# Feed-forward stages: token mean and 1/deviation as high/low product pairs, sums earlier in VectorE's order

## What is computed

```python
def _layernorm(x, axis=-1, eps=1e-05):
    m = jnp.mean(x, axis=axis, keepdims=True)
    v = jnp.var(x, axis=axis, keepdims=True)
    return (x - m) / jnp.sqrt(v + eps)

x_prev = jnp.concatenate([jnp.zeros((B, 1, C), x.dtype), x[:, :-1, :]], axis=1)
xr = mu_r * x + (1.0 - mu_r) * x_prev
xk = mu_k * x + (1.0 - mu_k) * x_prev
r = jax.nn.sigmoid(jnp.einsum('btc,dc->btd', xr, W_r))
k = jnp.einsum('btc,dc->btd', xk, W_k)
k_act = jnp.square(jax.nn.relu(k))
out = r * jnp.einsum('btc,dc->btd', k_act, W_v)

x = x + 0.5 * ffn(_layernorm(x))        # ffn_phase "ffn1"
x = x + attention(_layernorm(x))
x = x + 0.5 * ffn(_layernorm(x))        # ffn_phase "ffn2"
```

## Time and profile before

| | |
|---|---|
| median of 3 runs | 3531.27 us (3527.9 to 3531.66) |
| profiled execution | 3538.78 us |
| its span, first to last instruction | 3536.9 us |
| mean granted clock of TensorE | 0.972 of full |
| busy over the span: PE, DVE, ACT, POOL | 93%, 78%, 45%, 52% |
| matmuls, DVE, ACT, POOL instructions | 83236, 4491, 2344, 1707 |

### The profile page before, as it was taken

The page is one execution under the profiler, slowest core; times in us unless marked ns, Lnnn a source line. Parts: engine busy times, 40 slices in busy tenths (PEclk is TensorE's granted clock), DMA queues, the critical chain, the costliest instruction groups (busy, mean ns, idle before and its releaser), DMA issues. The chain is left out here.

```text
span 3536.9 us, 191423 instructions
## 1 busy us (share of the span) xinstructions
PE 3288.2 (93%) x83236; PEld 2760.8 (78%) x83236; DVE 2753.6 (78%) x4491; ACT 1583.4 (45%) x2344; POOL 1823.7 (52%) x1707
## 2 busy tenths in 40 slices
PE   7999998799999999995999999999996987999999
PEld 5888886576767767674999999999995765888887
DVE  6767775787888878784899999999997856676765
ACT  4455553577777777772112211221113433545454
POOL 1232322566555665654777888888874431223232
PEclk8999999899999999997999999999998998999999
DMA  3122212232323323225777777777774772212121
GB/s 119 71 97 81 101 77 95 74 99 82 103 73 92 93 74 99 86 76 133 187 198 199 200 199 199 203 201 197 200 197 149 228 221 99 107 71 107 71 107 59
DMA packets 486525, 452.84 MB, mean 128 GB/s; under 512 B 55488, under 2 KB 448832, under 8 KB 467264
## 3 DMA queue, kind: packets, MB, share of 16 engines
q1 hardware_dynamic: 484160, 449.56, 42.0%
q10 hardware_dynamic: 2304, 2.49, 0.3%
HBM read 331.33 MB, written 120.60 MB: 128 GB/s over the span
## 5 line engine op out<-in xcount | busy, mean ns | idle before, releaser
L350 POOL TENSOR_TENSOR ffn_out<-ffn_gate,ffn_xres 128x512 f32<-128x512 f32 x128 | 182.1, 1451 | 784.2 <-DVE ffn_gate L254 783.8
L784 DVE SCALAR_TENSOR_TENSOR ain_conv<-ain_padded,ain_taps,ain_conv 128x512 f32<-128x512 f32 x384 | 416.5, 1085 | 13.8 <-DVE ain_tail L781 0.3
L1464 ACT ACTIVATE rec_u<-rec_ps_end 128x256 f32<-128x256 f32 x128 | 49.2, 384 | 631.0 <-PE rec_ps_end L1516 631.0
L885 POOL TENSOR_TENSOR ain_conv<-ain_conv,ain_term 128x512 f32<-128x512 f32 x192 | 272.3, 1418 | 16.0
L1232 POOL TENSOR_TENSOR rec_d_norm<-rec_dmat,rec_early 128x512 f32<-128x512 f32 x128 | 162.7, 1271 | 174.8 <-DVE rec_dmat L1314 174.8
L940 ACT ACTIVATE ain_buf<-ain_conv 128x512 f32<-128x512 f32 x192 | 121.0, 630 | 232.3 <-POOL ain_conv L885 146.7
L46 PE MATMUL ffn_ring<-ffn_mixkh,ffn_wkh 128*128 128x512 f32 x512 | 218.4, 427 | 6.5 <-DVE ffn_mixkl L196 6.5
L46 PE MATMUL ffn_ring<-ffn_mixrh,ffn_wrh 128*128 128x512 f32 x512 | 215.4, 421 | 9.2 <-DVE ffn_mixrl L306 9.2
L46 PE MATMUL ffn_ring<-ffn_mixkh,ffn_wkl 128*128 128x512 f32 x512 | 203.2, 397 | 0.0
L46 PE MATMUL ffn_ring<-ffn_mixrh,ffn_wrl 128*128 128x512 f32 x512 | 202.0, 395 | 0.0
L46 PE MATMUL ffn_ring<-ffn_act_h,ffn_wvh 128*128 128x512 f32 x512 | 201.8, 394 | 0.0
(11 more groups left out here) (249 smaller groups left out, 10285.6 us busy)
## 6 DMA issues: line engine op xcount, KB each, us to landing
rec_early<-coeffs SPq DMA_DIRECT2D x512, 128.0 KB, 3.0
streams<-ain_buf SPq DMA_DIRECT2D x48, 1024.0 KB, 5.1
rec_qkv<-streams SPq DMA_DIRECT2D x126, 384.0 KB, 3.3
rec_qk_pe<-streams SPq DMA_DIRECT2D x127, 256.0 KB, 3.4
rec_late<-coeffs SPq DMA_DIRECT2D x504, 64.0 KB, 2.3
ffn_xres<-in_x SPq DMA_DIRECT2D x16, 1024.0 KB
ain_x<-x SPq DMA_DIRECT2D x16, 1024.0 KB, 4.9
gate<-ain_gate SPq DMA_DIRECT2D x16, 1024.0 KB, 6.7
```

The lines of the kernel that those rows point to most:

```text
L350: added = nc.gpsimd.tensor_tensor(out[:, m, :], gate[:, m, :], xres[:, m, :], ALU.add)
L784: nc.vector.scalar_tensor_tensor(out=out[:], in0=pad[:, n:n + TOK], scalar=taps[:, u // KT, u % KT, n:n + 1], in1=out[:], op0=ALU.mult, op ...
L885: nc.gpsimd.tensor_tensor(out[:], out[:], term[:], ALU.add).then_inc(pool_conv, 1)
L1464: nc.scalar.activation(u[:], ps_end[:, :, 1, :], ACT.Copy).then_inc(u_ready, 1)
```

## The change

The mean (from tile 2 on) and the spread of 1/deviation (all tiles) become two `float32r` matmuls each. Their moving operand is split into a high and a low part, and the constant operand is a `float32r` copy. ACT rounds `sum1` into `sum_h`, between its roundings of mix r and mix k; DVE subtracts. The four reciprocals per partition are split by two small DVE instructions, and the diagonal tile is twice as wide. DVE's `sums` goes ahead of `act_rest` 3, and the new `sum_rest` stands where `sums` stood.

```diff
+            dve.wait_ge(consts, 1)
+            nc.vector.tensor_copy(mean_r[:], mean_w[:])
+            nc.vector.tensor_copy(ones_r[:], ones[:])
...
+            def sum_rest(t):
+                dve.wait_ge(sum_high, t - 1)
+                nc.vector.tensor_tensor(sum_l[:], sum1[:], sum_h[:].bitcast(F32), ALU.subtract).then_inc(sum_split, 1)
...
                 dve.wait_ge(inverted, t + 1)
-                nc.vector.tensor_tensor(rstd_diag[:], ident[:].unsqueeze(1).to_broadcast([P, KT, P]),
-                                        rstd_tok[:].unsqueeze(2).to_broadcast([P, KT, P]), ALU.mult).then_inc(diagonal, 1)
+                nc.vector.tensor_copy(rstd_split[:, 0, :], rstd_tok[:]).then_inc(rstd_high, 1)
+                dve.wait_ge(rstd_high, t + 1)
+                nc.vector.tensor_tensor(rstd_split[:, 1, :], rstd_tok[:], rstd_split[:, 0, :].bitcast(F32),
+                                        ALU.subtract).then_inc(rstd_low, 1)
+                dve.wait_ge(rstd_low, t + 1)
+                nc.vector.tensor_tensor(rstd_diag[:], ident[:].unsqueeze(1).unsqueeze(1).to_broadcast([P, 2, KT, P]),
+                                        rstd_split[:].bitcast(F32).unsqueeze(3).to_broadcast([P, 2, KT, P]),
+                                        ALU.mult).then_inc(diagonal, 1)
...
                 act_rest(t, 2)
+                if ahead == 2:
+                    sums(t + 2)
                 act_rest(t, 3)
                 if ahead:
                     mix_rest(t + 1, "r", 0)
                 if ahead == 2:
-                    sums(t + 2)
+                    sum_rest(t + 2)
...
+            def sum_round(t):
+                act.wait_ge(summed, t)
+                act.wait_ge(mean_done, t)
+                nc.scalar.activation(sum_h[:], sum1[:], ACT.Copy).then_inc(sum_high, 1)
...
             def mean(t):
-                pe.wait_ge(summed, t)
-                nc.tensor.matmul(ps_mean[:], mean_w[:], sum1[:], start=True, stop=True).then_inc(mean_done, 1)
+                if isinstance(t, int) and t == 1:
+                    pe.wait_ge(summed, 1)
+                    nc.tensor.matmul(ps_mean[:], mean_w[:], sum1[:], start=True, stop=True).then_inc(mean_done, 1)
+                else:
+                    pe.wait_ge(sum_split, t - 1)
+                    nc.tensor.matmul(ps_mean[:], mean_r[:], sum_h[:], start=True, stop=False)
+                    nc.tensor.matmul(ps_mean[:], mean_r[:], sum_l[:], start=False, stop=True).then_inc(mean_done, 1)
...
-                nc.tensor.matmul(ps_rstd[:], ones[:], rstd_diag[:].rearrange("p j n -> p (j n)"), start=True,
-                                 stop=True).then_inc(spread, 1)
+                for part in range(2):
+                    last = nc.tensor.matmul(ps_rstd[:], ones_r[:], rstd_diag[:, part].rearrange("p j n -> p (j n)"),
+                                            start=(part == 0), stop=(part == 1))
+                last.then_inc(spread, 1)
```

More of the change, by code:

```diff
@@ L90, in ffn_phase @@
         var_tok, std_tok, rstd_tok = (sb(n, [P, KT]) for n in ("var_tok", "std_tok", "rstd_tok"))
-        rstd_diag = sb("rstd_diag", [P, KT, P])
+        rstd_diag = sb("rstd_diag", [P, 2, KT, P], F32R)
+        rstd_split = sb("rstd_split", [P, 2, KT], F32R)
+        sum_h, sum_l = sb("sum_h", [P, TOK], F32R), sb("sum_l", [P, TOK], F32R)
+        mean_r, ones_r = sb("mean_r", [P, P], F32R), sb("ones_r", [P, P], F32R)
         ps_mean = ctx.enter_context(nc.psum_tensor(f"{tag}_mean", [P, TOK], F32))
@@ L108, in ffn_phase @@
         v_used, out_ready = sem("v_used"), sem("out_ready")
+        sum_high, sum_split, rstd_high, rstd_low = sem("sum_high"), sem("sum_split"), sem("rstd_high"), sem("rstd_low")
         x0_loaded, r_loaded = [sem(f"x0_loaded{k}") for k in range(2)], sem("r_loaded")
@@ L407, in slot @@
                     high(t + 1, "r", 0)
+                if more == 2:
+                    sum_round(t + 2)
                 if more:
@@ L438, in _ @@
             high(0, "k", 1)
-            with act.Fori(0, NT - 1) as t:
-                slot(t, True)
-            slot(NT - 1, False)
+            with act.Fori(0, NT - 2) as t:
+                slot(t, 2)
+            slot(NT - 2, 1)
+            slot(NT - 1, 0)
         @block.tensor
```

## The result

The changed kernel takes 3540.59 us in the median of 20 runs, the kernel before 3529.07 us in 20 runs beside them. The ratio is 1.0023, 95% interval [1.0016, 1.0029]: slower by 5.6 to 10.2 us, with 8.1 in the middle. The forecast was +8.4 us and 3539.7.

What follows compares the result with a forecast made beforehand. PE was taken to bound a feed-forward slot; 23.5 us spared, 30.0 of new waits and 1.9 at the starts gave +8.4 us on the 3531.3 median, 3539.7 us. The range was 3533 to 3546.

Steps and rivals of the forecast that it cites:

- Matmuls: Mean and spread on PE: two float32r matmuls cost 0.46 us instead of 0.86, sparing 23.5 us in all.
- The reciprocal's chain: DVE between var and spread: two more steps and a wider diagonal, 0.95 us more, hidden in the loop.
- The start of each phase: At each feed-forward phase's start the 0.95 us of longer DVE chain is paid in full: 1.9 us.
- The sums, moved: Sums ahead of DVE's fourth low part make PE wait 1.07 us in effect in 28 slots: 30.0 us.
- Sum: Both feed-forward phases together: -23.5 + 30.0 + 1.9 = +8.4 us, or 3539.7 us against the median.
- the first rival: PE stays the bound if the moved sums fit into DVE's slack: -21.6 us, 3509.7 us; chance 0.08.
- The clock: PE's clock falls to 1.2 GHz at each new wait: 45 us in 28 slots, 3585; chance 0.04.
- The spread is not late: Rival: a slower cast or diagonal makes PE wait before the spread, 17 us more, 3557; chance 0.08.
- The near-cancelling case: The 0.11 behind PE's waits unpaid and the starts hidden: +3.4 us, 3534.7; inside the main case's 0.80.

Runs made afterwards that it cites:

- the kernel without the wait: The changed kernel with both sums moved directly behind the fourth low part of the activation: ratio 0.9941, 3513.36 us.
- half of the sums early: The changed kernel with only the first of the two sums ahead of the fourth low part, the second behind it: ratio 0.9958.
- longer chain: The changed kernel with sums behind the fourth low part, plus three dependent 128x4 multiplications in DVE's chain of the reciprocal: ratio 0.9971.

## Why the prediction was right, point by point

- *Matmuls.* 0.405 us was taken for each mean and each spread. The slots of the two single-pair kernels show 0.40 and 0.39 (35.61 to 35.21 and 35.22), and those of both pairs 0.81. The pair's matmuls start 0.23 us apart (216.31 and 216.54), as the row of before had it. The Trainium skill, page "TensorE: Matmul & The Clock Gate", section "Back-to-back issue gap", gives 216 ns for 512 columns at full clock as the distance of single matmuls, and about 131 ns for a stream in which each has its weight load, as here. The rows have 229; the measurement decides.
- *The reciprocal's chain.* The cast has 0.17 us and the steps are 0.20 apart (0.21 was taken), the diagonal 1.23 (1.22 was taken). It ends 0.39 us ahead of the spread, and three more steps make PE wait as the slack says.
- *The start of each phase.* 0.95 us was taken. From the L200 of before to the first L282 it was 3.81 us (16.12 to 19.93), and it is 4.74 in the changed kernel (16.33 to 21.07): 0.93. PE's first wait grows from 4.6 to 5.5. What of this reaches the total is less sure. Outside the loops the two phases took 1.3 us more, where my terms make 1.9 - 2 x 0.405 = 1.1; but the run with a plain first tile gained nothing. The starts scatter by more than the term: the run with the mean's pair alone has the first tile's chain of before, and its first `normalise` stands at 53.50, not 54.85. In the stretch from 50 to 60 us its granted clock was 1.00, before it was 0.84.
- *The sums, moved.* 1.07 us of wait in effect was taken, and 35.88 us for the slot. Measured: 35.885 less the 34.80 of the kernel without the wait is 1.08. Of this the record shows 0.79 as idle, some 0.16 lie under the recorded end of the matmul before, and 0.11 in the first matmul behind it. My text expected some 0.95 of idle: there I forgot that a matmul's recorded end lies 0.16 behind the next one's possible start.
- *Sum.* -23.5 + 30.0 + 1.9 = +8.4 us was forecast; the ratio gives +8.1, interval 5.6 to 10.2, and the two phases in the trace +8.7. The time itself is right by some luck: 3539.7 was added to a median of 3531.3 over three runs, while the 20 runs of before beside the changed kernel have 3529.07. That both 3539.7 and 3540.59 are over 3538.3, the line to "slower", is a matter of 1 or 2 us; I had given "slower" 0.58 and "within 0.2%" 0.32.
- *The rivals.* PE did not stay the bound; it does once the sums stand behind, at 0.9941 where the first rival had -21.6 us, 0.9939. The clock did not fall at a wait of this size. The spread is not late. The near-cancelling case (+3.4) lies below the interval, and the trace shows the 0.11 behind the wait as paid, 3.1 us of the 5 that this case leaves out.

What stays open: why the code between the phases, the same in all kernels, takes from 2312.9 to 2324.2 us from one execution to another, and whether the 1.9 us at the starts are paid in the total.

## What to carry to other kernels

Idle time of an in-order engine does not mean that work can be put anywhere in its order: DVE was idle for almost 30% of a slot, but work put ahead of the one instruction that the bound engine was about to need, with 0.97 us of slack, cost what it exceeded this by and some 0.1 us on top. Before moving work, find the next result that the bound engine takes from that queue and measure its slack; here the same work was free one instruction later, and the change then gave -0.6% instead of +0.2%. In a loop, read the distance between repeats of one instruction: it resolves 0.02 us per slot where whole runs scatter by several, and it shows waits that the list of waits hides.

## What the runs showed of the hardware that I had not expected

- Waits of PE of 0.24 and 0.25 us between matmuls (half of the sums early, longer chain) had no line in the view of waits. Each cost 0.11 us more than itself: behind the first, a matmul took 0.34 us in place of 0.23; behind the second, the pair took 0.57 in place of 0.46.
- A wait of 1.93 us once per slot brought PE down to 1.2 GHz in every third slot (from 142.37 to 145.8 in the one shown), at 1.6 us each. Waits of 0.79 us never did in 28 slots, and in the third phase of the kernel before one of 1.64 us did not the earlier trace rows. Since 20 of the 28 waits of 1.93 us did not either, the wait's length alone does not decide it.
- The distance from a DVE instruction to the next depended on whether the next one waited for it by a semaphore: 1.25 us for a 128x1024 addition with such an instruction behind it, 1.14 without. In a term of half a microsecond that is a fifth.
